# The turning transfers are issued by ACT instead of SP

## The reference

```
h = LN(LN(x; pw gain, offset by token id); cp gain, offset by kind)
t = LN(x; tm gain, offset by kind)      s = LN(x; ms gain, offset by scale)
m, n, r = x + one small MLP row per batch (three of them)
cat = [w0*h, w1*t, w2*m, w3*n, w4*r, w5*s]          w = softmax(aw)
x1 = x + LN(silu(cat @ W1 + b1) @ W2 + b2; g, b)
y  = (x1 * style) @ W.T * demod, plus bias, clipped to +-256;   out = x1 + y
```

## Time and profile before

| what | value |
|---|---|
| median of 3 runs | 1145.07 us (1144.97 to 1145.15) |
| profiled execution | 1145.62 us, its span 1143.8 us |
| TensorE busy | 1123.7 us (98%) |
| DVE busy | 946.7 us (83%) |
| ACT busy | 694.5 us (61%) |
| DMA queues | 28.4% of 16 engines' span on q1, 14.2% on q0 |

### The profile page before, as it was taken

How to read it: one execution, slowest core, us unless ns; L and a number is a source line. 1 busy time by engine, 2 the same in 40 slices (tenths; PEclk the granted TensorE clock), 3 DMA queues, 4 the chain that set the end, 5 groups by cost and what they waited for, 6 DMA issues and landing times.

```text
span 1143.8 us, 14853 instructions
## 1 busy us (share of the span) xinstructions
PE 1123.7 (98%) x4977; PEld 917.3 (80%) x4977; DVE 946.7 (83%) x1772; ACT 694.5 (61%) x987; POOL 245.9 (21%) x269
## 2 busy tenths in 40 slices
PE   5999999999999999999999999999999999999998
PEld 4667888888888888888888888888888888888887
DVE  7898989879797897979789797897979789797846
ACT  4647575574756648475674846658475673846653
POOL 3451222113121221222113122211222112122000
PEclk9999999999999999999999999999999999999999
DMA  9962354343525335263443635334362433525102
GB/s 322 355 193 61 95 160 114 109 97 107 154 83 142 91 109 133 84 169 97 114 96 101 155 83 147 106 103 119 86 178 85 133 78 113 142 83 140 45 1 74
DMA packets 130300, 138.90 MB, mean 121 GB/s; under 512 B 84624, under 2 KB 85264, under 8 KB 130128
## 3 DMA queue, kind: packets, MB, share of 16 engines
q1 hardware_dynamic: 114800, 86.99, 28.4%
q0 software_dynamic: 14336, 50.34, 14.2%
q10 hardware_dynamic: 1088, 0.62, 0.2%
HBM read 101.74 MB, written 16.78 MB: 104 GB/s over the span
## 4 chain that ended last, share of the span: by engine, by line
PE 90%; DVE 3%; SPq 2%; DMA 2%; ACT 1%; issue 1%; POOL 0%; DVEq 0%; POOLq 0%; ACTq 0%
PE pre L1304 14%; PE pre L1308 14%; PE pre L1311 14%; PE uy L1362 5%; PE uy L1365 5%; PE uy L1363 5%; PE uy L1375 5%; PE uy L1378 5%; PE uy L1376 5%; PE pre L1343 5%; PE pre L1344 5%; PE pre L1342 5%; PE turn L1284 2%; SPq L297 2%; DMA early_hi_x<-mlp_w 2%; PE pre L1325 1%
## 5 line engine op out<-in xcount | busy, mean ns | idle before, releaser
L462 POOL TENSOR_TENSOR ra<-vea,half 128x1 f32<-128x1 f32 x64 | 45.0, 703 | 475.3 <-DVE vea L878 475.3
L627 ACT ACTIVATE hi_a<-xT,style 128x512 fp32r<-128x512 f32 x60 | 43.5, 725 | 137.0 <-DVE xT L984 137.0
L444 POOL DMA_INDIRECT gb<-pw_table,pw_ids x63 | 77.8, 1235 | 107.6 <-DMA tmp_c<-gb 86.8
L1365 PE MATMUL uy<-lo_c,w_hi_w 128*128 128x512 f32 x256 | 100.0, 391 | 0.3 <-DVE lo_c L937 0.2
L1362 PE MATMUL uy<-hi_c,w_hi_w 128*128 128x512 f32 x256 | 100.1, 391 | 0.0
L1363 PE MATMUL uy<-hi_c,w_lo_w 128*128 128x512 f32 x256 | 100.0, 390 | 0.0
L1342 PE MATMUL pre<-hi_b,w_hi_x 128*128 128x512 f32 x256 | 99.8, 390 | 0.0
L1344 PE MATMUL pre<-lo_b,w_hi_x 128*128 128x512 f32 x256 | 99.6, 389 | 0.0
L1343 PE MATMUL pre<-hi_b,w_lo_x 128*128 128x512 f32 x256 | 99.6, 389 | 0.0
L1375 PE MATMUL uy<-hi_a,w_hi_l 128*128 128x512 f32 x240 | 93.9, 391 | 0.0
L1378 PE MATMUL uy<-lo_a,w_hi_l 128*128 128x512 f32 x240 | 93.4, 389 | 0.0
(11 more groups left out here) (268 smaller groups left out, 2968.4 us busy)
## 6 DMA issues: line engine op xcount, KB each, us to landing
xT<-x_turned SPq DMA_DIRECT2D x64, 256.0 KB, 3.0
out_turned<-xT SPq DMA_DIRECT2D x63, 256.0 KB, 2.6
xt<-x_in SPq DMA_DIRECT2D x62, 256.0 KB, 2.6
sel_in<-sel_ids SPq DMA_DIRECT2D x16, 192.0 KB, 4.0
raw_s<-int_w SPq DMA_DIRECT2D x2, 512.0 KB
raw_h<-int_w SPq DMA_DIRECT2D x1, 1024.0 KB, 22.8
early_hi_w<-mlp_w SPq DMA_DIRECT2D x1, 1024.0 KB, 20.0
raw_w<-mlp_w SPq DMA_DIRECT2D x1, 1024.0 KB, 22.2
```

Of the source, the lines that this page charges most:

```text
L1365: last = pe.matmul(bank, w_hi["w2"][:, c, cut], lo["c"][:, c, :], start=False, stop=c == C - 1)
```

## The change

`turn_tile` moves from SP's block to ACT's. All its calls leave SP's loop and stand in ACT's order: for tiles 4 and 5 behind their `part_halves`, for the fourth tile of each group behind its `part_halves`, for the third of the next group the same, and for the first and second of the next group one after the other behind `hidden(i, 3)`. It waits for the same semaphores as before. `turn_rows` stays on SP.

```diff
--- before.py
+++ after.py
@@ -325,15 +325,6 @@
             def store(i, c):
                 sp.wait_ge(y_done, i * C + c + 1)
                 sp.dma_start(out[c * P:(c + 1) * P, i * GROUP:(i + 1) * GROUP], xT[:, i % 2, c, :]).then_inc(out_stored[c], 16)
-
-            def turn_tile(t):
-                i, j = t // TPG, t % TPG
-                sp.wait_ge(halves_apart, t - TPG + 1)
-                if j < 2 or (j == 2 and i > 1):
-                    sp.wait_ge(pre_ready, i * C)
-                else:
-                    sp.wait_ge(u_ready, i * C)
-                sp.dma_start_transpose(turned(t).rearrange("p (g k) -> p g k", k=P), apart(t)).then_inc(halves_turned[j], 16)
 
             def turn_rows(i):
                 sp.wait_ge(e_ready, (i + 1) * TPG)
@@ -385,7 +376,6 @@
                     load_sel(i + 1)
                     if i:
                         load_xt(f + 1)
-                        turn_tile(f - 1)
                     load_xt(f + 2)
                     if i:
                         store(i - 1, 0)
@@ -397,22 +387,13 @@
                         store(i - 1, 2)
                         load_xT(i + 1, 1)
                     if i == 0:
-                        turn_tile(f)
-                        turn_tile(f + 1)
-                    if i == 0:
                         load_xt(f + 4)
-                        turn_tile(f + 2)
                     if i:
                         store(i - 1, 3)
                         load_xT(i + 1, 2)
                         load_xT(i + 1, 3)
-                        turn_tile(f)
-                        turn_tile(f + 1)
                         if i + 2 < GROUPS:
                             load_xt(f + 4)
-                        turn_tile(f + 2)
-                else:
-                    turn_tile(i * TPG + 3)
             i = GROUPS - 1
             for c in range(C):
                 store(i - 1, c)
@@ -558,6 +539,15 @@
                 act.wait_ge(gate_done, t + 1)
                 nc.scalar.activation(apart(t).rearrange("p (s d) -> p s d", s=2), gb_tile(t)[:, 1, :].bitcast(U16).rearrange("p (d s) -> p s d", s=2),
                                      ACT.Copy).then_inc(halves_apart, 1)
+
+            def turn_tile(t):
+                i, j = t // TPG, t % TPG
+                act.wait_ge(halves_apart, t - TPG + 1)
+                if j < 2 or (j == 2 and i > 1):
+                    act.wait_ge(pre_ready, i * C)
+                else:
+                    act.wait_ge(u_ready, i * C)
+                act.dma_start_transpose(turned(t).rearrange("p (g k) -> p g k", k=P), apart(t)).then_inc(halves_turned[j], 16)
 
             def join_halves(t):
                 turn_landed(act, t)
@@ -723,12 +713,14 @@
             split_rows(1)
             gate(5)
             part_halves(4)
+            turn_tile(4)
             act.wait_ge(b2_ready, 1)
             filled(act, "dcoef")
             u_out(0, 0)
             split_t(1, 0)
             u_out(0, 1)
             part_halves(5)
+            turn_tile(5)
             add_be(0, 0)
             split_t(1, 1)
             add_be(0, 1)
@@ -746,6 +738,7 @@
                 if i == 1:
                     gate(t + 2)
                     part_halves(t + 2)
+                    turn_tile(t + 2)
                 split_h(i, 0)
                 join_halves(t + 1)
                 split_s(i, 1)
@@ -758,6 +751,7 @@
                 split_s(i, 2)
                 gate(t + 3)
                 part_halves(t + 3)
+                turn_tile(t + 3)
                 if i == 1:
                     add_be(0, 3)
                     split_s(i, 3)
@@ -791,6 +785,9 @@
                 if more:
                     join_rows(n)
                 hidden(i, 3)
+                if more:
+                    turn_tile(n * TPG)
+                    turn_tile(n * TPG + 1)
                 add_be(i, 2)
                 if more:
                     split_rows(n)
@@ -801,6 +798,7 @@
                     gate(n * TPG + 2)
                     split_t(n, 0)
                     part_halves(n * TPG + 2)
+                    turn_tile(n * TPG + 2)
                 u_out(i, 2)
                 if more:
                     split_t(n, 1)
```

## The result

The changed kernel takes 1192.37 us (median of 4 runs, 1191.72 to 1192.60) against 1145.02 us for the kernel before on the same chip: a ratio of 1.0413, 95% interval 1.040 to 1.0425. It is 47.3 us slower; the forecast was 39.3 us slower, at 1184.3 us, within a range of 1150 to 1204.

The account below looks back on a forecast made before the run. TensorE, busy 68.00 of 68.00 us in a steady group, was taken as the bound; 2.02 + 0.58 = 2.60 us over 14 groups (36.4) plus 2.8 at the start gave 39.2 us, so 1184.3 us, range 1150 to 1204.

Parts of the forecast that it names:

- The bound and the sign: TensorE never stops from the second group on, so earlier transfers win nothing; slower 0.86, same 0.11, faster 0.03.
- What one issue costs: A turning transfer on ACT's queue takes 1.24 us to issue, two in a row 2.60 us, as on SP.
- the smaller meeting with SP's plain issues: ACT's issues meeting SP's plain ones add up to 0.4 us a group: 1190 us; no chance of its own.
- The dearer: Rival: an ACT issue at 1.80 us, 31 us more in all: 1216 us; chance 0.08 for above 1200.
- the cheaper rival: ACT issues at 0.41 us: 1145 to 1147 us, chance 0.11; at medium 0.8 us: 1160 us, chance 0.21.
- Step 1: Pair behind hidden(i, 3): split_rows 1.49 us late; TensorE gets the bank from u_out(i, 0) 0.65 us late.
- the rival of the early start: The pair's issue starts with hidden(i, 3)'s last copy, at 570.79, otherwise as forecast: 1180.8 us; chance 0.15.
- Step 2: Third transfer, before u_out(i, 2): 2.90 us late against 0.88 slack; gain 2.02 late, 0.65 of them from Step 1.
- Step 3: Fourth transfer, behind part_halves(t+3): DVE 2.30 us late, statistics' turn has 1.50 slack; hidden(i, 3) 0.58 late each group.
- The sum: 2.60 us a group, 14 groups, 36.4 us, plus 2.8 us at the start: 39.2 us together.
- The waits foretold: TensorE waits each group: 0.4 to 1 us for ug, some 1.4 for tmp_a, short for lo_c; DVE's over 1.5.

Follow-up runs that it names:

- e2: Against the kernel before, only the third turning transfer of each group is issued by ACT, the others stay on SP: 1159.82 us (ratio 1.0128).
- e7: Against the kernel before, ACT issues the pair and the third transfer of each group, the fourth stays on SP: 1181.21 us (ratio 1.0315).
- e4: Against the kernel before, no transfer moved; ACT makes two unread copies wherever the change issues a turning transfer: 1190.62 us (ratio 1.0401).
- e3: Against the kernel before, only the fourth turning transfer of each group is issued by ACT, the others stay on SP: 1149.00 us (ratio 1.0034).
- e6: Against the changed kernel, ACT's issues stand at other places of its order, tiles 4 to 7 kept: 1150.42 us (ratio 1.0049).
- e1: Against the kernel before, only the pair of each group is issued by ACT, third and fourth stay on SP: 1159.01 us (ratio 1.0124).
- e5: Against the kernel before, turning transfers stay on SP; ACT issues a small plain transfer (16 bytes a partition) at each changed place: 1149.86 us (ratio 1.0049).

## Why the prediction was right, point by point

**The bound and the sign.** Right. TensorE had no gap to close, and each late value became a stop.

**What one issue costs.** Right: on ACT 1.249 us (median of the 44 for `whole_b`), forecast 1.24. The pair was a little dearer, 2.70 to 2.86 us in the 14 groups, forecast 2.60: the smaller meeting with SP's plain issues that stood among the rivals (last section). The dearer and the cheaper rival both fell with this.

**Step 1.** Forecast 0.65 us; in the group shown TensorE lost 0.48 at the gain, 0.20 at the third unit of u and 0.11 in the matmul behind it, 0.79 in all. The issue began at 594.79, 0.07 after the last copy's start (594.72): the early end of the 0.25 us that I had left open. So the rival of the early start was the true one, and by it alone the forecast would have been 1180.8 us and step 1 0.40 us. Other sizes made up for it: the pair took 2.77 for 2.60 us and the last copy itself was 0.18 us late against TensorE, so `split_rows` came 1.64 us late for 1.49; and the gain began 0.15 and not 0.04 us after DVE's `rows` was done. That the middle value came so near is partly luck. The rule of the Trainium skill (page "Perfetto Trace Analysis", section "Per-instruction lifecycle: what the profiler-reported window actually captures"), that ACT's operations wait in a queue of their own while the sequencer goes on to the DMA, agrees with this row.

**Step 2.** Forecast 1.37; measured 1.33 and 0.11 in the matmul behind it. From the first matmul of unit u on, `u_out(i, 2)` starts 13.56 us in, before 10.47 (580.30 - 569.83, where 569.83 is that matmul's start before): 3.09 late, where 2.90 and step 3's 0.58 had been forecast. e2 and e7 show the mechanism, one shared slack.

**Step 3.** The mechanism was right, the size was off, and this is the worst of the three. Forecast 0.58 us in every group; in the group shown the statistics' turn is issued 1.91 us later against TensorE than before (3.96 us ahead of unit u, before 5.87), where I had 2.30; `join_rows` waits for its landing (0.34 us, for `root<-sq`) and is 0.44 late, not 0.80, and TensorE loses only 0.10 at the end of the first unit of u. In four groups (1, 2, 14 and one between) the turn lands from 0.04 us ahead of unit u to 0.69 behind its start, and not 0.8 ahead, and that costs TensorE a wait of 0.4 to 1.1 us. What I had passed over is DVE's order behind the late `low_h(i, 2)`: `low_s(i, 2)` stands right behind it, and TensorE stops for it:

```profile
PEld pre L1309 <- DVE lo_b L922: 5.8, 14, 0.6
```

That is 14 weight loads held 0.4 us each, worth 0.2 to 0.4 us of TensorE's time a group (0.30 and 0.11 behind it in the group shown). The forecast had looked at the h, x1 and x halves behind this place and not at the s halves. The wait comes only where enough lateness adds up: it is there in the changed kernel and in e4, and not in e3 (the fourth alone) nor in e7 (the pair and the third). By size the two errors nearly cancel in a steady group (0.10 and 0.41 for 0.58), which is luck.

**The sum.** Forecast 2.60 us a group. In the group shown the stops add to 2.74 (0.10, 0.79, 1.44 and 0.41) and its distance grew by 2.91 (68.30 to 71.21); the average over eleven is 2.87. The matmul after each stop starts 0.34 us and not 0.227 us before the next one, so each stop costs 0.11 us more than the wait: three or four stops a group, and no term of the sum had it. The larger part of the missing 8 us is at the edges. Forecast for the start 2.8 us, and for groups 1, 2 and the last no more than for any other; measured 3.7 at the start, and 8.1 and 3.7 for three groups that the sum had at 7.8. At the start tile 4's issue cost 0.43 us, which I had at nothing, and the two stops behind the issues of tiles 5 and 6 1.67 and 1.37, forecast 1.4 each. In the three groups most of the excess is the late statistics' turn of step 3. The forecast also said that the last group issues nothing; it issues tile 63's transfer.

**The waits foretold.** TensorE's for `tmp_a` (1.17 us shown) and DVE's for ACT's `rows` (2.14) came as written. TensorE's first stop stands one matmul ahead of the one foretold, at the gain, for DVE's `rows`; the one for `ug` behind it showed only among the weight loads, and the one for `lo_c` is too short for the view. That TensorE's busy time would stay at 1124 us was wrong (1142.5), as told above, and its share fell to 96% and not 95%.

## What to carry to other kernels

Issuing a transfer is work of the engine's queue: moving it from an idle queue to one that feeds the bound costs its issue time (here 1.25 us, and up to 0.13 around it) at that place, less the slack there. Look for the first value behind the new place that the bounding engine reads, and subtract; then add up all that is put ahead of the same value, since they share one slack (0.68 + 0.84 us became 2.12). Where an issue has to be on a busy queue, put it where that queue idles anyway: the same 60 issues cost 47 us or 5.

## What the runs showed of the hardware

ACT's issue may start well ahead of its arithmetic, if it waits for nothing new. In e6, an issue that stands behind `split_t(i, 3)` in ACT's order began 0.59 us before that instruction did:

```profile
588.66 0.63 ACT L530 ACTIVATE hi_a<-tmp_a 128x512 fp32r<-128x512 f32 x1
588.73 1.25 ACTq L550 DMA_TRANSPOSE whole_b<-gb  x1
590.08 1.37 ACT L555 ACTIVATE whole_c<-whole_b 128x1024 uint16<-128x1024 uint16 x1 [0.78 <-issue]
590.72 1.25 ACTq L550 DMA_TRANSPOSE whole_b<-gb  x1
591.31 0.60 ACT L530 ACTIVATE hi_a<-tmp_a 128x512 fp32r<-128x512 f32 x1
```

So the second issue was hidden beside the join of 1.37 us, and only the first one left ACT idle, for 0.78 us. In the changed kernel the wait for ACT's own copy forbids this: the issue at 605.83 comes 0.03 us after the copy's end.

After an issue ACT's next instruction started 0.05 us (behind the pair and the fourth) to 0.10 us (before `u_out`) later.

The two engines' issues do disturb each other a little. In e1, where SP's loads of `xT` are issued at about the same time as ACT's pair, six pairs had no issue of SP beside them and took 2.62 to 2.63 us, seven had one and took 2.76 to 3.18, and one (2.65) began just behind one:

```profile
301.28 2.62 ACTq L568 DMA_TRANSPOSE whole_b<-gb  x2
...
989.99 2.35 SPq L318 DMA_DIRECT2D xT<-x_turned  x2
991.86 3.18 ACTq L568 DMA_TRANSPOSE whole_b<-gb  x2
```

All 14 pairs of the changed kernel had one beside them (2.70 to 2.86 us), and in each the second issue was the longer one (1.35 to 1.51 us, the first 1.25 to 1.27). With plain issues in ACT's queue (e5), the 32 turning transfers of SP that started together with one took 1.49 us to issue and the 30 without one 1.25 (medians). Why the second issue of a pair is the longer one, no run shows.

Nor does any run show what makes tile 6's issue at the start long: 1.25 us in the changed kernel, and 1.9 to 2.5 us in all the others and before, on whichever engine. Had it been as long in the changed kernel, the start would have cost more: in e6, where tiles 4 to 7 stand as in the change, it took 2.37 us and the stop behind it cost 2.48 us, for 1.37 in the changed kernel.
